# Absorbed products of head pairs behind all row turns, and a third buffer for the fused products' loads

## The reference

```python
x = x + _L0_attn_ref(_layernorm(x))        # q[l,n,c]; scores over the 4 samples n, for each of 1024 columns l
...
q = _rmsnorm(x @ wq_a.T, q_a_ln_w) @ wq_b.T          # second layer's attention, 32 heads, 64 + 64 wide
kv = _rmsnorm(ckv, kv_a_ln_w) @ wkv_b.T              # per head 64 (k_nope) + 128 (v)
...
out @ wo.T
```

## Time and profile before

| | before |
|---|---|
| median of 3 runs | 1657.12 us (1654.94 to 1658.3) |
| profiled execution, its own time | 1656.97 us |
| its span on the core | 1655.2 us |
| PE busy | 1565.7 us, 95% |
| DVE busy | 1022.9 us, 62% |
| ACT busy | 870.8 us, 53% |
| POOL busy | 811.7 us, 49% |
| DMA, mean over the span | 151 GB/s |

### The profile page before, as it was taken

How to read it: one execution, slowest core, us unless ns; L and a number is a source line. 1 busy time by engine, 2 the same in 40 slices (tenths; PEclk the granted TensorE clock), 3 DMA queues, 4 the chain that set the end, 5 groups by cost and what they waited for, 6 DMA issues and landing times. The chain is left out here.

```text
span 1655.2 us, 32088 instructions
## 1 busy us (share of the span) xinstructions
PE 1565.7 (95%) x12430; PEld 963.7 (58%) x12430; DVE 1022.9 (62%) x2763; ACT 870.8 (53%) x1670; POOL 811.7 (49%) x699
## 2 busy tenths in 40 slices
PE   6998799999888999999999999989999999999998
PEld 5764455555554777777677777644444444465554
DVE  6796866777767888888888888833111010254433
ACT  6786312221667999999999999942210000111110
POOL 4221444445764888888888888840010000144440
PEclk9899899999999999999999999999999999999999
DMA  9696424443664999999999999988863331223331
GB/s 321 208 333 230 89 64 128 128 140 101 143 127 99 173 185 189 174 184 189 213 183 182 186 176 175 184 173 205 225 169 80 102 89 26 67 55 92 82 92 64
DMA packets 559752, 249.32 MB, mean 151 GB/s; under 512 B 502256, under 2 KB 535152, under 8 KB 559216
## 3 DMA queue, kind: packets, MB, share of 16 engines
q1 hardware_dynamic: 559600, 247.26, 65.3%
HBM read 73.15 MB, written 48.23 MB: 73 GB/s over the span
## 5 line engine op out<-in xcount | busy, mean ns | idle before, releaser
L1887 POOL TENSOR_TENSOR xb<-xb 128x1280 f16<-128x1280 f32 x128 | 335.7, 2623 | 7.9 <-ACT xb L1773 7.9
L1765 ACT ACTIVATE xb<-so,D_sv,qw_c 128x512 f32<-128x512 f32 (+3 forms) x512 | 289.4, 623 | 3.2 <-DVE D_sv L1830 3.1
L1821 DVE TENSOR_REDUCE so<-so 128x1 f32<-128x512 f32 (+3 forms) x512 | 228.0, 491 | 18.6 <-PE so L1717 17.8
L92 POOL TENSOR_SCALAR mv<-mv 128x1 f32<-128x1 f32 x64 | 31.3, 490 | 293.5 <-DVE mv L87 293.3
L1773 ACT ACTIVATE xb<-xb 128x1280 f16<-128x1280 f32 x128 | 162.7, 1271 | 14.7 <-DMA xb<-xb 11.0
L2012 DVE SCALAR_TENSOR_TENSOR xb<-so,ms_c,xb 128x512 f32<-128x512 f32 x32 | 22.6, 747 | 227.6 <-PE so L50 227.6
L1708 PE MATMUL so<-kTh,D_QTh 128*128 128x512 f16 (+3 forms) x512 | 153.5, 300 | 9.0 <-ACT xb L1765 8.7
L1709 PE MATMUL so<-kTl,D_QTh 128*128 128x512 f16 (+3 forms) x512 | 153.2, 299 | 0.0
L1710 PE MATMUL so<-kTh,D_QTl 128*128 128x512 f16 (+3 forms) x512 | 146.5, 299 | 0.0
L1893 POOL TENSOR_TENSOR D_qs<-D_qs,D_t 128x256 f32<-128x256 f32 x128 | 93.1, 727 | 89.6 <-DVE D_t L1854 89.6
L1732 PE MATMUL D_t<-vh,xb 128*128 128x65 f16 x1280 | 131.4, 194 | 4.5 <-DVE D_on L1840 4.5
(11 more groups left out here) (307 smaller groups left out, 4212.0 us busy)
## 6 DMA issues: line engine op xcount, KB each, us to landing
A_wo<-in_wo SPq DMA_DIRECT2D x16, 1024.0 KB, 6.0
od<-D_os SPq DMA_DIRECT2D x32, 512.0 KB, 4.2
mwd<-A_mst SPq DMA_DIRECT2D x32, 256.0 KB, 2.7
xd<-xb SPq DMA_DIRECT2D x16, 512.0 KB, 4.1
ow_raw<-mwd SPq DMA_DIRECT2D x16, 512.0 KB, 5.4
xb<-xd SPq DMA_DIRECT2D x16, 512.0 KB, 6.1
out_x<-xb SPq DMA_DIRECT2D x16, 512.0 KB, 3.1
xb<-in_x SPq DMA_DIRECT2D x6, 1024.0 KB, 15.6
```

What stands on the lines that cost most here:

```text
L1765: m = e.activation(p[:, AT[i]:AT[i] + N], Sb[n % 4][:, c:c + N], ACT.Exp, scale=qw.col(qw.NEG, g), bias=s[:, 7 - i:8 - i])
L1821: m = e.tensor_reduce(minima(u, i), Sb[n % 4][:, c:c + N], AX.X, ALU.min)
L1887: e.tensor_tensor(P2[u % 3][:, 1280:2560], P[u % 3][:, :], P2[u % 3][:, 0:1280], ALU.subtract).then_inc(s_pl, 1)
```

## The change

In the first layer's step, for the work on weights beside it:

- The absorbed products are made for pairs of heads: a matmul contracts over 128 rows, which hold the query weights of two heads, against a 128 x 128 block that holds their two key weights on its diagonal and zeros beside them. A group has 8 matmuls of 128 columns instead of 16 of 64. The loads go to 128 partitions instead of 64; `wuk` has twice the bytes. The result is the same.
- `a0` no longer stands behind row turn 11. All side work begins behind the turns, in the order `a0`, `a1`, `f0`, `a2`, `f1`, `a3`. ACT has it among its squares and exponentials, in an order that is written out. `f(k)` stands in the chunks where `f(k-1)` stood, and the last, `f15`, behind message (6, 1).
- `wo` has a third buffer, in the half of `N_room` that `wqn` no longer takes. Three loads of `wo` are issued at the start, and the load for `f(k)` behind the stores of `f(k-3)`. Both first groups are loaded behind all of x.

```diff
-    wqn = [room[0:64, 2048 * i:2048 * i + 2048].rearrange("p (h n) -> p h n", h=8) for i in range(2)]
-    wuk = [room[0:64, 4096 + 512 * i:4608 + 512 * i].rearrange("p (h n) -> p h n", h=8) for i in range(2)]
+    wqn = [room[:, 1024 * i:1024 * i + 1024].rearrange("p (h n) -> p h n", h=4) for i in range(2)]
+    wuk = [room[:, 4096 + 512 * i:4608 + 512 * i].rearrange("p (h n) -> p h n", h=4) for i in range(2)]
-    wo = [ph.sb(f"wo{i}", [128, 2, D]) for i in range(2)]
+    wo = [ph.sb(f"wo{i}", [128, 2, D]) for i in range(2)] + [room[:, 2048:4096].rearrange("p (h d) -> p h d", h=2)]
...
-    SIDE_LN = {11: "a0"}
-    SIDE_MID = ("a1", "a2", "f0")
-    SIDE_J = {(0, 0): "a3", (0, 1): "f1", (0, 3): "f2", (1, 0): "f3", (1, 2): "f4", (2, 0): "f5", (2, 2): "f6", (3, 0): "f7", (3, 2): "f8",
-              (4, 0): "f9", (4, 2): "f10", (5, 0): "f11", (5, 2): "f12", (6, 0): "f13", (6, 1): "f14", (6, 2): "f15"}
+    SIDE_MID = ("a0", "a1", "f0", "a2", "f1", "a3")
+    SIDE_J = {(0, 1): "f2", (0, 3): "f3", (1, 0): "f4", (1, 2): "f5", (2, 0): "f6", (2, 2): "f7", (3, 0): "f8", (3, 2): "f9",
+              (4, 0): "f10", (4, 2): "f11", (5, 0): "f12", (5, 2): "f13", (6, 0): "f14", (6, 1): "f15"}
...
-                for h in range(8):
-                    i = e.matmul(wb[k][:, 64 * h:64 * h + 64], wqn[G % 2][:, h, 128 * k:128 * k + 128], wuk[G % 2][:, h, :],
+                for h in range(4):
+                    i = e.matmul(wb[k][:, 128 * h:128 * h + 128], wqn[G % 2][:, h, 128 * k:128 * k + 128], wuk[G % 2][:, h, :],
...
-                w.wait_ge(s_wo[kt % 2], 16 * (kt // 2 + 1))
+                w.wait_ge(s_wo[kt % 3], 16 * (kt // 3 + 1))
...
-        for n in range(4):
-            square(0, n, n)
-        side(SIDE_MID[0])
+        square(0, 0, 0)
+        square(0, 1, 1)
+        absorbed(0)
+        square(0, 2, 2)
+        square(0, 3, 3)
+        absorbed(1)
         exps(0)
         weigh(0)
-        side(SIDE_MID[1])
-        side(SIDE_MID[2])
+        fused(0)
+        absorbed(2)
         for n in range(4):
             square(1, n, 4 + n)
         exps(1)
+        fused(1)
+        absorbed(3)
...
-            if kt + 2 < 16:
-                load_wo(kt + 2)
+            if kt + 3 < 16:
+                load_wo(kt + 3)
...
-            if t == 10:
-                load_group(0)
+        load_group(0)
+        load_group(1)
         e.dma_start(cst[:, C_COS:C_MEAN], a["cst"][:, C_COS:C_MEAN]).then_inc(s_k, 16)
...
-        load_group(1)
-        e.dma_start(wv[:, :, :], a["wv"]).then_inc(s_v, 16)
-        load_wo(0)
-        load_wo(1)
+        w.wait_ge(s_id, 16)
+        e.dma_start(wv[:, :, :], a["wv"]).then_inc(s_id, 16)
+        for kt in range(3):
+            load_wo(kt)
```

More of the change, by code:

```diff
@@ L563, in first @@
     s_x = ph.sems("x", 10)
-    s_id, s_k, s_v = ph.sem("id"), ph.sem("k"), ph.sem("v")
-    s_g, s_wo, s_mst = ph.sems("g", 2), ph.sems("wo", 2), ph.sems("mst", 4)
+    s_id, s_k = ph.sem("id"), ph.sem("k")
+    s_g, s_wo, s_mst = ph.sems("g", 2), ph.sems("wo", 3), ph.sems("mst", 4)
     s_tr, s_hT = ph.sem("tr"), ph.sem("hT")
@@ L584, in staged @@
     def staged(kind, k, half_):
-        first_ = {"a": (0, 2, 4, 8)[k]} if kind == "a" else {"f": 8 + 2 * k if k else 6}
-        return first_[kind] + half_
+        at = (0, 2, 6, 10)[k] if kind == "a" else (4, 8)[k] if k < 2 else 8 + 2 * k
+        return at + half_
     def x_landed(w, t):
@@ L609, in fused @@
             for hf in range(2):
-                w.wait_ge(s_wo[kt % 2], 16 * (kt // 2 + 1))
-                w.wait_ge(s_v, 16)
+                w.wait_ge(s_wo[kt % 3], 16 * (kt // 3 + 1))
+                w.wait_ge(s_id, 32)
                 w.wait_ge(s_me, 2 * kt + hf - 1)
                 for hh in range(2):
-                    i = e.matmul(mb[hf][64 * hh:64 * hh + 64, :], wv[:, 2 * kt + hh, :], wo[kt % 2][:, hh, 512 * hf:512 * hf + 512],
+                    i = e.matmul(mb[hf][64 * hh:64 * hh + 64, :], wv[:, 2 * kt + hh, :], wo[kt % 3][:, hh, 512 * hf:512 * hf + 512],
                                  start=True, stop=True)
@@ L645, in pe @@
                 i.then_inc(s_tr, 1)
-            side(SIDE_LN.get(t))
         for work in SIDE_MID:
@@ L884, in load_group @@
             w.wait_ge(s_wp, 2 * (G - 2) + 2)
-            e.dma_start(wuk[G % 2][:, :, :], a["wuk"][:, 8 * G:8 * G + 8, :]).then_inc(s_g[G % 2], 16)
-            e.dma_start(wqn[G % 2][:, :, :], a["wqn"][:, 8 * G:8 * G + 8, :]).then_inc(s_g[G % 2], 16)
+            e.dma_start(wuk[G % 2][:, :, :], a["wuk"][:, 4 * G:4 * G + 4, :]).then_inc(s_g[G % 2], 16)
+            e.dma_start(wqn[G % 2][:, :, :], a["wqn"][:, 4 * G:4 * G + 4, :]).then_inc(s_g[G % 2], 16)
         def load_wo(kt):
-            w.wait_ge(s_mp, 2 * (kt - 2) + 2)
-            e.dma_start(wo[kt % 2][:, :, :], a["wo"][256 * kt:256 * kt + 256, :].rearrange("(h j) d -> j h d", j=128)).then_inc(s_wo[kt % 2], 16)
+            w.wait_ge(s_mp, 2 * (kt - 3) + 2)
+            e.dma_start(wo[kt % 3][:, :, :], a["wo"][256 * kt:256 * kt + 256, :].rearrange("(h j) d -> j h d", j=128)).then_inc(s_wo[kt % 3], 16)
         def absorbed(G):
@@ L924, in sp @@
         e.dma_start(lnr[:, :], a["lnr"].partition_broadcast(128)).then_inc(s_k, 16)
-        load_group(1)
-        e.dma_start(wv[:, :, :], a["wv"]).then_inc(s_v, 16)
-        load_wo(0)
-        load_wo(1)
-        for t in range(NT):
-            side(SIDE_LN.get(t))
+        w.wait_ge(s_id, 16)
+        e.dma_start(wv[:, :, :], a["wv"]).then_inc(s_id, 16)
+        for kt in range(3):
+            load_wo(kt)
         for work in SIDE_MID:
@@ L2422, in layout @@
     wqb = i["L1_attn_wq_b"].reshape(32, 128, 256)
-    o["wqn"] = c(wqb[:, :64].transpose(1, 0, 2))
+    o["wqn"] = c(wqb[:, :64].reshape(16, 2, 64, 256).transpose(1, 2, 0, 3).reshape(128, 16, 256))
     o["wpe"] = c(wqb[:, 64:][:, deint].reshape(8, 256, 2, 128).transpose(0, 3, 2, 1))
     wkvb = i["L1_attn_wkv_b"].reshape(32, 192, 64)
-    o["wuk"] = c(wkvb[:, :64].transpose(1, 0, 2))
+    wuk = np.zeros((2, 64, 16, 2, 64), np.float32)
+    for x in range(2):
+        wuk[x, :, :, x, :] = wkvb[x::2, :64].transpose(1, 0, 2)
+    o["wuk"] = wuk.reshape(128, 16, 128)
     o["wv"] = c(wkvb[:, 64:].transpose(1, 0, 2))
```

## The result

| | before | after |
|---|---|---|
| median | 1657.33 us (1654.94 to 1658.3, 4 runs) | 1643.41 us (1641.45 to 1643.77, 4 runs) |
| ratio to before | | 0.9918, 95% interval 0.9897 to 0.994 |
| profiled execution, its own time | 1656.97 us | 1643.77 us |
| its span | 1655.2 us | 1642.0 us |
| PE, DVE, ACT busy | 1565.7, 1022.9, 870.8 us | 1551.3, 1022.6, 869.4 us |

The change makes the kernel 13.9 us faster. The forecast was 12.0 us and 1645.0. DVE and ACT do what they did; only TensorE lost busy time.

A forecast was written before the change was run, and what follows sets the result against it. DVE was taken to set the pace until chunk 6, then TensorE's waits for `wo`. Gains of 3.5 us at the start and 8.5 at the end made 12.0 off 1656.97, so 1645.0; range 1642.0 to 1650.0.

The forecast's parts named there:

- the case forecast: Whole kernel: 12.0 us gained, 1645.0 us; chance 0.60, with a range of its own from 1642.8 to 1647.5.
- The turns without `a0`: Row turns at the start: they keep their old pace, so `hT` is whole at 39.6, 3.8 us earlier.
- The new groups: Absorbed products on TensorE: a group of 16 records takes 2.1 us at full clock, 3.9 at half clock.
- the rival that they are not cheaper: Absorbed groups keep 3.78 and 7.09 us; the start gains only 0.3 us, time 1648.2; chance 0.12.
- Group 2: Load for `a2`, issued at about 43.2: lands between 49.1 and 52.0, taken as 50.0 us.
- The bound of 52.0: Latest landing of the load for `a2`, if it queues behind a third `wo` load: gain 10.0 us, time 1647.0.
- The clock of `a2`: `a2` on TensorE after its load wait: half clock as before, so 3.9 us, from 50.0 to 53.9.
- ScalarE's queue behind the exponential: Chunk 1: `f1` and `a3` delay ACT's weighing, DVE waits some 2 us; start gains 3.5 us, not 5.7.
- The end: Behind chunk 5: waits for `wo` go with three buffers, message (7, 0) ends at 155.0; 8.5 us gained.
- What follows: Next step behind message (7, 0): nothing has a time of its own, so all 12.0 us is passed on.
- The range: Whole kernel: 1642.0 to 1650.0 us, the upper end covering the rivals that lose the start.

The follow-up runs named there:

- the pairs alone: The kernel before with only the paired absorbed products and their wider loads, in the old order with two `wo` buffers: median 1647.96 us, ratio 0.994.
- the unused matmuls: The kernel before plus 20 matmuls of 128 columns with unread results in TensorE's idle time ahead of `a2`: median 1653.54 us, ratio 0.9991.
- the columns of 64: The changed kernel with each pair's matmul cut into two of 64 columns over the same 128 rows: median 1649.57 us, ratio 0.9957.
- the repeat: The changed kernel measured a second time with nothing changed: median 1641.86 us, ratio 0.9912.

## Why the prediction was right, point by point

The time, 1643.4 against 1645.0, lies inside the range, and the case forecast is the one that came. By its steps:

- **The turns without `a0`**: forecast 3.8 us earlier, measured 3.74 in T. Confirmed. The first product is at 40.10 and not 39.7 since the first turn began 0.4 us later (10.31 against 9.92). The reason was only half right, though: the pairs alone give 3.2 of it with `a0` left in its place. A group of 1.95 us fits nearly whole between two turns. The old one did not, neither at 5.50 us (T 33.53) nor, ahead of the unused matmuls, at 3.78 (T 33.79, with the turns behind it at the low clock).
- **The new groups**: forecast 2.1 us at full clock, measured 1.95 to 2.05. Confirmed, and this refutes the rival that they are not cheaper; the columns of 64 show that it is the number of matmuls that counts.
- **Group 2**: forecast landing 50.0, `a2` began at 49.28. The bound of 52.0 assumed that the loads of `wo` land as late as in the earlier trace rows. They don't:

```profile
L894 SPq DMA_DIRECT2D A_wo<-in_wo x2: 765/1241/1717, 22.2 to 23.0; - x2
...
DMA to landing us min/median/max: 14.6/15.5/16.4
```

   Issued at 22.2 and 23.0, they were there by 23.0 + 16.4 = 39.4, and the third, issued at 24.8, by 41.9. Nothing of them was ahead of group 2, issued at 43.5. The 52.0 had stood beside the Trainium skill, DMA: Bandwidth & Descriptors, section Queues, rings and completion order, by which each DMA engine takes the descriptors of a queue in order. With no `wo` ahead of group 2 the changed kernel does not test that.
- **The clock of `a2`**: assumed low, 3.9 us; it was 1.00, and `a2` took 2.05. This is the term that was off. L768 came at 56.46 without a wait and not at 57.6 with one, and the start gained 4.7 us and not 3.5. But the clock is not given by the program: in the repeat `a2` began at 48.45 and took 3.31 us, and L came out the same to 0.04 us. ScalarE's idle time ahead of the exponential took it up; it was 1.21 us there and not 2.36. So what was over-priced is not only the clock but what hangs on it: a slow `a2` of 3.31 us cost L nothing.
- **ScalarE's queue behind the exponential**: forecast DVE waiting some 2 us for the weighing of chunk 1; it waited 2.07. Confirmed; message (0, 0) was not waited for.
- **The end**: forecast 8.5, measured 8.40. The number and the wait for ScalarE ahead of `f15`, forecast at 146.6 − 145.5 = 1.1 us and measured at 1.36, are confirmed. The attribution was wrong: I gave it to the third buffer. Two buffers in the new order have the same E. And some 4 of the 8.5 us were waits and a low clock of the one execution that I read; against the 18.26 us of the other execution, whose end has the code of before, the change gains 4.3. That the number fits is in so far luck: the forecast and the measured E are taken against the same execution.
- **What follows**: "all is passed on" failed by 1.0 us of the 14.24. N rose by 1.5 us, with the first tiles of the next step at a lower granted clock than in other variants; that this is the cause is likely and not shown.
- **Between**: L gained 2.49 us where the steps, after T, had none. Of the 5.84 us gained at message (6, 0) 4.7 were there by the weighing of chunk 1. Of the other 1.1, 0.7 is the length of that weighing, 1.41 us and not 2.09 as in the earlier trace rows, and 0.4 the product right behind it, 0.69 us at 62.85 and not 1.10. Why both took longer before is open. The product, before:

```profile
68.24 1.10 DVE L757 CUSTOM_DVE_ANT_0 N_room<-F_room 128x512 f32<-128x512 f32 x1
```

   and the weighing for the last chunk in the changed kernel:

```profile
138.26 1.33 ACT L703 ACTIVATE A_h<-F_room,A_ex 128x512 f32<-128x512 f32 x2 [0.86 <-DVE A_ex L786]
```

   This weighing (in the earlier trace rows at 144.12) is 5.86 us earlier, the same as message (6, 0). Nothing was lost in the chunks between: DVE sets the pace there, as read from the earlier trace rows.
- **The range.** The lower end of the forecast case, 4.4 and 9.6 us gained, is 1643.0 and not 1642.8; the measured time lies inside either way.

## What to carry to other kernels

Count small f32 matmuls by their number before their columns: with weights of its own a record of 64 columns cost nearly as much as one of 128 here (0.118 and 0.122 to 0.128 us), so packing two heads on a diagonal halved the time although half of the products are with zeros. When a change joins a cheaper operation, a new order and more buffers, try each alone before carrying the three on together; here the first gave two thirds of the median, and the others removed partly the same waits. And cut the program at a few events that each variant has, and compare the stages: spans of the changed kernel moved by 2 us between executions, its stages by 0.04. But profile both sides twice before trusting a stage: the end of the kernel before was 22.3 us in one execution and 18.3 in another with the same code there.

## What the hardware showed that was not expected

- The spread goes with the clock as well. The kernel before ran in 1649.56 to 1667.11 us over the comparisons, the changed one in 1640.93 to 1643.77. The 12 runs with the unused matmuls ahead of `a2` go from 1649.37 us at a mean granted clock of 0.991 to 1658.15 at 0.984. Which causes which is not shown, and what makes the clock fall in one execution and not in the next stays open.
- The same loads land at quite different times. In the execution of before the first two loads of `wo` took 21.6 and 22.4 us to landing; with the unused matmuls, where the program is the same up to there, 26.9 and 27.7. At the end of the layer it was the other way round, 8.1 to 8.4 and 5.2 to 5.7.
- In the kernels with pairs these first two loads took 13.7 to 17.3 us, and without pairs in the new order 19.2 and 20.6. That does not show quicker loads into 128 partitions: without pairs they were issued earlier and landed at 37.6 and 40.1, with pairs and two buffers at 36.0 and 38.6. Only in the old order without pairs do they land clearly later (41.5 and 45.3).
